# Opening and closing of a software pipeline written out tile by tile, a new order for its regular tick, and one addition moved from VectorE to GpSimd

## What is computed

```python
x = x + 0.5 * ffn(layernorm(x))        # ternary weights, d_ff 512
x = x + attn(layernorm(x))             # eight layers, below
x = x + 0.5 * ffn(layernorm(x))
# ffn(x):  h = gelu(ternary_linear(x, w_up));  return ternary_linear(h, w_down)
# ternary_linear(x, w): x / rms(x) @ ternary(w).T
# a layer of attn, for sequences of 256 tokens:
#   Q, K = elu(x Wq + bq) + 1, elu(x Wk + bk) + 1;  value = x Wv + bv
#   V = Q * sum(K * value) / (Q * sum(K) + eps)
#   x = ln(gelu(V Wo + bo) + x);  x = ln(gelu(gelu(x W1 + b1) W2 + b2) + x)
```

## Time and profile before

| | us |
|---|---|
| median of three runs | 927.53 |
| the profiled execution, its own time | 928.71 |
| its span, first to last instruction | 926.9 |
| busy: PE, DVE, ACT, POOL | 855.2, 823.6, 795.8, 443.4 |
| mean granted TensorE clock | 0.959 |

### The profile page before, as it was taken

The page is one execution under the profiler, slowest core; times in us unless marked ns, Lnnn a source line. Parts: engine busy times, 40 slices in busy tenths (PEclk is TensorE's granted clock), DMA queues, the critical chain, the costliest instruction groups (busy, mean ns, idle before and its releaser), DMA issues.

```text
span 926.9 us, 14284 instructions
## 1 busy us (share of the span) xinstructions
PE 855.2 (92%) x3915; PEld 601.6 (65%) x3915; DVE 823.6 (89%) x3349; ACT 795.8 (86%) x1138; POOL 443.4 (48%) x561
## 2 busy tenths in 40 slices
PE   3898469999999999999999999999999999985897
PEld 2788245666666666666666666666666666654786
DVE  6677567999999999999999999999999999966663
ACT  3784579999999999999999999999999999733871
POOL 3253512555555555555555555555555555333230
PEclk8799789999999999999999999999999999995998
DMA  5000000000000000000000000000000000000011
GB/s 153 1 8 3 27 0 10 1 15 1 21 1 16 13 10 0 15 13 10 3 14 21 1 15 0 21 1 16 12 0 1 1 1 1 1 0 1 24 35 35
DMA packets 19518, 12.04 MB, mean 13 GB/s; under 512 B 1160, under 2 KB 18288, under 8 KB 19440
## 3 DMA queue, kind: packets, MB, share of 16 engines
q1 hardware_dynamic: 19440, 11.13, 4.2%
HBM read 9.03 MB, written 2.10 MB: 12 GB/s over the span
## 4 chain that ended last, share of the span: by engine, by line
DVE 69%; PE 12%; ACT 9%; issue 8%; POOL 2%; DMA 0%; DVEq 0%; ACTq 0%; POOLq 0%
DVE z L859 16%; DVE st L845 10%; DVE x_fm L1069 5%; DVE phi_k L982 5%; DVE kvf L993 4%; DVE phi_q L972 4%; DVE mv L852 4%; DVE e L965 4%; DVE vf L1034 3%; DVE x_hi L1077 3%; PE bank L544 3%; PE bank L394 2%; DVE y L1042 2%; ACT hsq L771 2%; ACT fh L764 2%
## 5 line engine op out<-in xcount | busy, mean ns | idle before, releaser
L1303 POOL TENSOR_TENSOR x_lo<-x_fm,x_hi 128x512 fp32r<-128x512 f32 x120 | 155.5, 1306 | 259.3 <-DVE x_hi L1077 259.3
L495 PE MATMUL bank<-h,w 128*128 128x512 f32 x512 | 260.5, 593 | 0.0
L737 ACT ACTIVATE h<-bank,par 128x512 f32<-128x512 f32 x256 | 167.1, 693 | 11.6 <-PE bank L402 10.6
L859 DVE TENSOR_SCALAR z<-bank,mv,rstd 128x128 f32<-128x128 f32 x512 | 169.2, 401 | 8.4 <-POOL rstd L1295 8.2
L400 PE MATMUL bank<-x_hi,w_hi 128*128 128x512 f32 x256 | 151.6, 592 | 1.6 <-ACT h L737 1.6
L1295 POOL TENSOR_TENSOR rstd<-ve,minus_half 128x4 f32<-128x4 f32 x128 | 132.8, 1037 | 10.7
L400 PE MATMUL bank<-x_hi,wqkv_hi 128*128 128x512 f32 x192 | 107.5, 560 | 11.2 <-DVE phi_q L972 10.1
L845 DVE BATCH_NORM_STATS2 st<-bank 128x6 f32<-128x128 f32 x512 | 112.8, 281 | 1.0 <-PE bank L394 0.9
L394 PEld LDWEIGHTS bank<-ident,y 128*128 128x128 f32 x512 | 62.3, 141 | 59.9 <-ACT x_fm L753 23.4
L402 PE MATMUL bank<-x_hi,w_lo 128*128 128x512 f32 x256 | 101.2, 395 | 0.0
L401 PE MATMUL bank<-x_lo,w_hi 128*128 128x512 f32 x256 | 101.1, 395 | 0.0
(11 more groups left out here) (102 smaller groups left out, 1780.7 us busy)
## 6 DMA issues: line engine op xcount, KB each, us to landing
x_tm<-in_x SPq DMA_DIRECT2D x8, 256.0 KB, 4.0
raw_w<-in_W SPq DMA_DIRECT2D x8, 256.0 KB, 2.7
w<-in_W SPq DMA_DIRECT2D x8, 256.0 KB, 2.9
out<-x_tm SPq DMA_DIRECT2D x8, 256.0 KB, 2.3
...
```

Of the source, the lines that this page charges most:

```text
L495: mm = pe.matmul(m.ps_o[:, :], m.w2[T.weights][:, c, :], m.h[:, T.par, c, :], start=c == 0, stop=c == FC - 1)
L737: act.activation(m.h[:, T.par, c, :], m.ps_h[c % 2][:, :], ACT.Gelu_apprx_tanh, bias=column(m, B1, T.layer, c, FC)).then_inc(s.gelu_h[T.pa ...
L859: last = dve.tensor_scalar(dst[:, j, :], src(j), mv[:, j, 0:1], scale[:, j:j + 1], ALU.subtract, ALU.mult)
L1303: pool.tensor_tensor(m.x_lo[:, T.slot, :], m.x_fm[:, T.slot, :], m.x_hi[:, T.slot, :].bitcast(F32), ALU.subtract).then_inc(done, 1)
```

## The change

The loop now runs for ticks 2 to 31. Ticks 3 to 30 are regular and hold layer steps only, in a new order on each engine and at new lags; the table loads on ACT follow from that order. Ticks 2 (OPENING) and 31 (CLOSING) are written out, tile by tile. OPENING holds the whole first FFN and the layer steps up to where tick 3 goes on (projections of jobs 0 to 7, `up` of job 3 in part); CLOSING holds the rest of jobs 56 to 63 and the whole last FFN. The second addition of the squares is a step of its own, `add_halves`, on POOL. Steps of jobs whose position isn't given by the regular tick also wait until the buffer that they write has been read (`reused`); it does this in ticks 2, 3, 4 and 31. Several FFN steps get such a wait too (`at_least` on a count of n-2). `split_first_qkv` and `split_first_w1` split the first layer's weights on POOL in the opening list. The transfers are unchanged. The full lists are long; what stands here are the regular lists and the places in the written-out ones that are spoken of.

```diff
@@ -12,10 +12,7 @@
 FC = 4
 FF = FC * P
 JOBS = LAYERS * NT
-TICKS = JOBS // 2
-TICKS_IN = NT // 2
-TICK_QKV, TICK_W1 = -29, -29
-FIRST_TICK, END_TICK = -34, 58
+OPENING, CLOSING = 2, 31
 KEY, QUERY, VALUE = 0, 1, 2
-    def __init__(self, job):
+    def __init__(self, job, loose=True):
         self.n = job + 1
+        self.loose = loose
         self.layer = job // NT
         self.weights = self.layer % 2
-def tiles_of(tick, f):
-
+def tiles_of(tick):
 
     def l(k, lag):
         job = 2 * (tick - lag) + k
-        return Tile(job) if 0 <= job < JOBS else None
-
-    def a(k, lag):
-        t = 2 * (tick - lag + TICKS_IN) + k
...
 
 def at_least(eng, sem, value):
 
     if value > 0:
...
+
+
+def reused(eng, T, sem):
+
+    if T.loose:
+        at_least(eng, sem, T.n - 2)
 
 
...
-    outer_up(a(0, -28), 3)
-    up(l(0, 2), 3)
...
-    project_o(l(0, 0))
-    outer_up(a(0, -29), 2)
+    fin, fout = f
+    if tick == OPENING:
+        outer_up(Outer(fin, 0), 0)
+        outer_up(Outer(fin, 0), 1)
+        outer_up(Outer(fin, 0), 2)
+        outer_up(Outer(fin, 0), 3)
+        outer_down(Outer(fin, 0), 0)
+        outer_down(Outer(fin, 0), 1)
+        turn(pe, m, Outer(fin, 1), left)
+        squares(Outer(fin, 0))
...
+        outer_up(Outer(fin, 7), 0)
+        outer_up(Outer(fin, 7), 1)
+        project(Tile(0), VALUE)
+        outer_down(Outer(fin, 6), 0)
+        outer_up(Outer(fin, 7), 2)
+        outer_up(Outer(fin, 7), 3)
+        outer_down(Outer(fin, 6), 1)
+        squares(Outer(fin, 6))
+        turn_c(Outer(fin, 3))
+        project(Tile(0), QUERY)
+        project(Tile(0), KEY)
+        outer_down(Outer(fin, 7), 0)
+        outer_down(Outer(fin, 7), 1)
...
+    elif tick == CLOSING:
+        turn_z(Tile(60), 0)
+        turn_z(Tile(57), 1)
+        up(Tile(59), 3)
+        project(Tile(63), VALUE)
+        turn_y(Tile(61), 0)
+        enter(Outer(fout, 0))
...
+        down(Tile(63), 1)
+        down(Tile(63), 2)
+        turn(pe, m, Outer(fout, 0), left)
+        down(Tile(63), 3)
+        enter(Outer(fout, 5))
+        outer_up(Outer(fout, 0), 0)
+        turn_z(Tile(62), 1)
...
+        outer_down(Outer(fout, 0), 0)
+        turn_z(Tile(63), 1)
+        outer_up(Outer(fout, 1), 2)
...
+        outer_up(Outer(fout, 7), 3)
+        squares(Outer(fout, 6))
+        outer_down(Outer(fout, 6), 0)
+        outer_down(Outer(fout, 6), 1)
+        squares(Outer(fout, 7))
+        outer_down(Outer(fout, 7), 0)
+        outer_down(Outer(fout, 7), 1)
+    else:
+        turn_z(l(0, 1), 0)
+        up(l(1, 2), 3)
+        turn_z(l(1, 3), 1)
+        project(l(1, 0), VALUE)
+        turn_y(l(0, 2), 1)
+        project(l(0, -1), KEY)
+        turn_y(l(1, 1), 0)
+        project(l(0, -1), QUERY)
+        down(l(1, 2), 0)
+        up(l(0, 1), 0)
+        down(l(1, 2), 1)
+        down(l(1, 2), 2)
+        project(l(0, -1), VALUE)
+        down(l(1, 2), 3)
+        project(l(1, -1), KEY)
+        project(l(1, -1), QUERY)
+        up(l(0, 1), 1)
+        up(l(0, 1), 2)
+        turn_z(l(1, 1), 0)
+        turn_z(l(0, 2), 1)
+        project_o(l(0, 0))
+        up(l(0, 1), 3)
+        turn_y(l(1, 2), 1)
+        down(l(0, 1), 0)
+        turn_y(l(0, 0), 0)
+        down(l(0, 1), 1)
+        project_o(l(1, 0))
+        up(l(1, 1), 0)
+        down(l(0, 1), 2)
+        up(l(1, 1), 1)
+        down(l(0, 1), 3)
+        up(l(1, 1), 2)
...
+    fin, fout = f
+    if tick == OPENING:
+        gelu(Outer(fin, 0), 0)
+        gelu(Outer(fin, 0), 1)
+        gelu(Outer(fin, 0), 2)
+        gelu(Outer(fin, 0), 3)
+        square(Outer(fin, 0))
+        normal(act, m, Outer(fin, 1))
+        z_hi(act, m, Outer(fin, 1))
...
+        gelu(Outer(fin, 7), 3)
+        square(Outer(fin, 7))
+        negative(Tile(0), KEY)
+        negative(Tile(0), QUERY)
+        exp(Tile(0))
+        enter_full(Outer(fin, 3))
+        enter_hi(Outer(fin, 3))
+        log_den(Tile(0))
...
+        negative(Tile(4), KEY)
+        log_den(Tile(2))
+        recip(Tile(2))
+        full(Tile(0), 0)
+        exp(Tile(4))
+        log_den(Tile(3))
+        recip(Tile(3))
+        gelu_h(Tile(0), 0)
...
+    else:
+        negative(l(0, -1), QUERY)
+        recip(l(0, 0))
+        exp(l(0, -1))
+        log_den(l(1, 0))
+        recip(l(1, 0))
+        gelu_h(l(0, 1), 0)
+        gelu_ff(l(1, 2))
+        negative(l(1, -1), KEY)
+        gelu_h(l(0, 1), 1)
+        gelu_h(l(0, 1), 2)
+        full(l(1, 1), 0)
+        gelu_o(l(0, 0))
+        negative(l(1, -1), QUERY)
+        gelu_h(l(0, 1), 3)
+        exp(l(1, -1))
+        gelu_o(l(1, 0))
+        gelu_h(l(1, 1), 0)
+        gelu_h(l(1, 1), 1)
+        gelu_ff(l(0, 1))
+        gelu_h(l(1, 1), 2)
+        full(l(0, 0), 0)
+        gelu_h(l(1, 1), 3)
+        log_den(l(0, -1))
+        negative(l(0, -2), KEY)
...
             return
+        reused(dve, T, (s.turned_y1, s.turned_y2)[i])
         dve.wait_ge((s.gelu_o, s.gelu_ff)[i], T.n)
...
     def add_squares(F):
         if not F:
             return
-        at_least(dve, F.f.ssq, F.n - 2)
         at_least(dve, F.f.hsum, F.n - 1)
         dve.wait_ge(F.f.hsq, F.n)
         dve.tensor_tensor(m.hss[:, :, :], m.hsq[:, 0:2, :], m.hsq[:, 2:4, :], ALU.add).then_inc(F.f.hss, 1)
-        dve.wait_ge(F.f.hss, F.n)
-        dve.tensor_tensor(m.hsum[:, F.par, :], m.hss[:, 0, :], m.hss[:, 1, :], ALU.add).then_inc(F.f.hsum, 1)
...
+        alpha(dve, m, Outer(fin, 4))
+        alpha(dve, m, Outer(fin, 5))
+        mean_square(Outer(fin, 1))
+        add_squares(Outer(fin, 2))
+        beta(Outer(fin, 1))
+        outer_residual(Outer(fin, 1))
...
+        z_c(Outer(fin, 5))
+        round_kq(Tile(0))
+        phi_q(Tile(0))
+        phi_k(Tile(0))
+        mean_square(Outer(fin, 7))
+        neg_ksum(Tile(0))
+        var_eps_c(Outer(fin, 6))
+        sum_kv(Tile(0))
...
+        outer_means(dve, m, Outer(fout, 3))
+        outer_stats(dve, m, Outer(fout, 5))
+        full(Tile(63), 1)
+        var_eps(dve, m, Outer(fout, 3))
+        add_squares(Outer(fout, 0))
...
+        beta(Outer(fout, 6))
+        add_squares(Outer(fout, 7))
+        outer_residual(Outer(fout, 6))
+        mean_square(Outer(fout, 7))
+        beta(Outer(fout, 7))
+        outer_residual(Outer(fout, 7))
+    else:
+        z(l(0, 3), 1)
+        mean_v(l(1, 1))
+        sum_kv(l(0, 0))
+        attend(l(1, 1))
+        residual(l(1, 3), 1)
+        hi(l(1, 2), 0)
+        full(l(0, 3), 1)
+        residual(l(0, 1), 0)
+        stats(l(1, 3), 1)
+        hi(l(0, 3), 1)
+        means(l(1, 3), 1)
+        sum_value(l(0, 0))
+        over_ksum(l(0, 0))
+        stats(l(0, 1), 0)
+        means(l(0, 1), 0)
+        z(l(1, 3), 1)
+        mean_v(l(0, 0))
+        z(l(0, 1), 0)
+        round_kq(l(1, 0))
+        residual(l(1, 1), 0)
+        phi_k(l(1, 0))
+        residual(l(0, 2), 1)
+        neg_ksum(l(1, 0))
+        full(l(1, 3), 1)
+        hi(l(0, 1), 0)
+        phi_q(l(1, 0))
+        sum_kv(l(1, 0))
+        over_ksum(l(1, 0))
+        hi(l(1, 3), 1)
+        stats(l(0, 2), 1)
+        stats(l(1, 1), 0)
+        sum_value(l(1, 0))
+        attend(l(0, 0))
+        means(l(1, 1), 0)
+        round_kq(l(0, -1))
+        means(l(0, 2), 1)
+        phi_k(l(0, -1))
+        phi_q(l(0, -1))
+        z(l(1, 1), 0)
+        neg_ksum(l(0, -1))
...
+    def add_halves(F):
+        if not F:
+            return
+        at_least(pool, F.f.ssq, F.n - 2)
+        pool.wait_ge(F.f.hss, F.n)
+        pool.tensor_tensor(m.hsum[:, F.par, :], m.hss[:, 0, :], m.hss[:, 1, :], ALU.add).then_inc(F.f.hsum, 1)
 
...
+    if tick == OPENING:
+        sd(Outer(fin, 0))
+        sd_eps(Outer(fin, 0))
+        split_first_qkv()
+        sd(Outer(fin, 1))
+        sd_eps(Outer(fin, 1))
+        sd(Outer(fin, 2))
+        sd_eps(Outer(fin, 2))
+        add_halves(Outer(fin, 0))
+        sd(Outer(fin, 3))
+        sd_eps(Outer(fin, 3))
...
+    else:
+        var_eps(l(0, 1), 0)
+        rstd(l(0, 1), 0)
+        low(l(0, 3), 1)
+        split_next_qkv(l(0, 0))
+        split_next_w1(l(0, 0))
+        split_next_qkv(l(1, 0))
+        split_next_w1(l(1, 0))
+        low(l(0, 1), 0)
+        low(l(1, 3), 1)
+        var_eps(l(1, 1), 0)
+        rstd(l(1, 1), 0)
+        var_eps(l(0, 2), 1)
+        rstd(l(0, 2), 1)
+        low(l(1, 1), 0)
+        var_eps(l(1, 2), 1)
+        rstd(l(1, 2), 1)
```

More of the change, by code:

```diff
@@ L423, in tensor_engine @@
     left.update(k=(s.par_kept, 1), v=(s.ternary_kept, 1), o=(s.ternary_kept, 2))
-    for tick in range(FIRST_TICK, END_TICK):
+    for tick in range(OPENING, CLOSING + 1):
         tensor_tick(pe, m, s, f, tick, left)
```

1153 lines of the change are left out of this document (896 added, 257 removed).

## The result

The changed kernel takes 898.72 us (median of four runs, 897.8 to 900.75), the kernel before 927.34 us beside it (926.24 to 928.54): ratio 0.969, 95% interval 0.968 to 0.971. That is 28.6 us less, where 884 was forecast. The profiled execution has a span of 899.0 us at a mean granted clock of 0.982 (before 926.9 and 0.959).

What follows compares the result with a forecast made beforehand. The prediction took PE and DVE as full in the middle, with idle time only at the ends; opening 150, middle 618.8 and closing 114 gave a span of 882.8 us, forecast as 884, range 860 to 910.

Steps and rivals of the forecast that it cites:

- The regular tick: Middle ticks, layer steps only: grow from 21.85 to 22.1 us, so 28 ticks cost 7 us more.
- The two waits of z for the root: DVE's regular tick: each z waits for POOL's reciprocal root, 0.14 and 0.09 us, both lengthening the tick.
- its upper end: Regular tick of 22.3 us if a POOL step also meets DVE steps on SBUF.
- The opening: First FFN and pipeline filling in one list: ACT bounds it, tick 3 on PE's ruler at 150 us instead of 178.
- The term up to the square of tile 7: Opening up to ACT's square of FFN tile 7: work at a rate of 0.87, square ending near 82 us.
- The term behind it: Opening after that square: ACT has 65 us of work, to 147, plus 8 for in-order waits, 155 on ACT.
- The closing: Last layer tiles and last FFN: DVE leads up to the last full, then PE's FFN work; 114 us instead of 137.6.
- The moved addition: Second addition of FFN squares, DVE to POOL: cost taken as 0, between -3 and +10 us.
- (B): Whole kernel: in-order lists stall more, 160 opening, ticks of 22.3, 122 closing; time 907 us, chance 0.2.
- A: Whole kernel as the terms sum: 150+618.8+114, time 884 us, own range 872 to 898, chance 0.54.
- (C): Whole kernel: lists work as written and roots arrive in time, 142+611.8+107; time 862 us, chance 0.2.
- (D): Both ends: slower because PE is kept at 1.2 GHz and its work costs double; 944 us with 60 us so, chance 0.05.

Runs made afterwards that it cites:

- e5: Changed kernel, DVE's regular tick reordered: mean_v of the first job between stats and means of the next first FF set, round_kq ahead of both z; 895.24 us.
- e6: Changed kernel with idle ACT copies of 512 columns added behind each negative step of the opening; ratio 0.9755.
- e7: Changed kernel with the first pass of K's and Q's product of the 8 opening tiles issued twice more on PE; ratio 0.9752.
- e4: Changed kernel, opening reordered: beta and residual of FFN tile 6 before tile 4's normalising, first layer tile's round_kq and phi steps earlier; ratio 0.968.
- e10: Changed kernel with an idle DVE addition of 512 columns behind each of the 11 layer-tile residuals in the closing; ratio 0.9775.
- e11: Changed kernel with the first pass of the 17 layer-tile up products in the closing issued twice more on PE; ratio 0.9739.
- e1: Changed kernel with the second addition of the FFN squares put back on DVE, right behind the first; 900.13 us.
- e3: Changed kernel, DVE's regular tick reordered: mean_v of the first job ahead of z of the second FF set, round_kq between the two z; ratio 0.968.
- e8: Changed kernel with an idle DVE addition of 512 columns behind each round_kq and phi_k of the opening's layer tiles; ratio 0.9707.
- e12: Changed kernel with e4's opening order, a further reordered DVE regular tick, and the last FFN tile's addition back on DVE; 895.71 us.
- e2: e1's kernel with 16 further idle POOL additions of constants at the same places, for which nobody waits; 915.1 us.

## Why the prediction was right and wrong

**What bounds the kernel.** Right: idle time was at the ends only, and both ends gave it, at nearly equal shares, 18.3 and 19.0 us. The middle gave back 9.5. But of the 44.1 us that the sum took off the span only 27.9 came.

**The regular tick.** Right in place and near in size: 22.18 measured for 22.1, a growth of 0.33 for 0.25. (That the middle comes within 0.9 us, 619.7 for 618.8, is in part luck: the sum counted 28 whole ticks, and the stretch is 1.3 us shorter than that.) The two waits of z for the root are there, 0.18 and 0.08 where 0.14 and 0.09 were worked out from the bare root chain. The third piece, 0.06 for a `round_kq` beside a POOL step, is of the kind that the prediction names for its upper end. As a cause the waits for the root are only half borne out: what it didn't foresee is that filling both brings 0.05 of their 0.26 us. In e5 the next step that needs ACT waits in their place, for an exp that ends 0.03 us ahead of it, so that a tick of 21.85 is not to be had by covering the roots alone.

**The opening.** The term up to the square of tile 7 was too long: it ends at 78.6 us, not 82 (+3.4 gained). The term behind it failed. "ACT has 65 us to do: 147, plus 8 for in-order waits", and 5.7 more up to the gelu: 78.7. It took 90.9, with 75.1 of ACT work and 15.8 of waits by the windows row 78.60:169.50. The work was under-priced by 4.4 us, the waits by 7.8, and 4.4+7.8-3.4 = 8.8 is the miss of 9.1 but for rounding. (One slip is in the prices: the parts named for an FFN tile on ACT add up to 7.0 to 7.4 us, not 6.7.) Under the larger term lies one step: I took ACT as the bound and added a few stalls to its work. By e6 and e7 the stretch fits a path through ACT and PE, and such a path can be longer than the work of either; that the clock has no part in it is not shown. The largest single wait, 3.7 us before the first log, came from DVE's list, where two normalisings of 1.1 and 2.0 us stand ahead of the first layer tile (e4); mending it brought 2.2 us on the spot and 1 to 1.5 us at the gelu.

**The closing.** DVE was rightly named (e10), with PE close behind (e11). DVE's first step of it came at 768.66, 0.8 us later than the forecast puts it against the gelu of tile 59 (10.4+11 us ahead of 789.22). From there to its last `full` at 836.1 it took 67.4 instead of 65 (60 of work, 5 of bare root chains): +2.4. From there to the end 62.9 us, where 48+4+1+4 = 57 and 3 for the clock were forecast: +2.9. Together this is the miss of 6.2 but for rounding. Its PE work is 55.8 at a granted clock of 0.90. The last product was forecast at 3.6 us; it took 5.45 at the lower clock, and 3.82 to 3.84 in e1, e3, e6, e7, e8 and e12. e3, e6, e7 and e8 have the changed kernel's list there, so it is not the list alone that decides it but when the clock falls: the 3.6 us were right only in some executions.

**The moved addition.** Forecast 0 within -3 to +10, measured 0.3 with 2 either way (e1). The number is right by luck, the reason is not. The prediction had both terms small: DVE not the bound, so that the 10 us buy little, and POOL with time to spare. The runs have both large: POOL's 16 additions cost 14 us where nobody waits for them (e1 to e2), and taking DVE's 16 away gives 14.6 (e2 to the changed kernel). On the last tile it costs 0.5 us (11.3 us from the last square's end to the end in e1 and e12, 11.8 in the four kernels with POOL's addition whose last product ran at the upper clock), for 0.65.

**The rivals.** (B), 907 with more stalls in order, came nearly true at the ends: of the 10 us that it set above A in the opening 9 came, of the 8 in the closing 6. In the middle it had ticks of 22.3, and 22.18 is a little nearer to A. (C), roots that come in time, is refuted by the two waits. (D), the clock: 0.92 from 78.6 to 169.5 us and 0.90 at the end, never a stretch at 0.50 of more than 7 us; refuted as a cause of the size that it needed. 898.7 lies between A and B, 8.3 us from B and 14.7 from A, and just outside A's own range (872 to 898). So the forecast holds in its bounds because they took in B; A as it was written, with hardly any waits beyond the 8 us, did not come.

**What would have shown it.** The tick was as named, and so was PE's share of the last 60 us but for the tail (47.6 of the 49.4 us from 836.1 to 885.5, 96% for 95). Projections began sooner than named, at 72.16 us for 75 to 80; the gelus at 169.5 and 789.2 and the 109.8 us behind them were each later than the 160, 779 and 104 named. "ACT under 85% busy from 82 us on points to B" did so: 83%. Neither sign of being wrong showed: the middle moved by 9.5 us, not 12, and no end gained under 10.
